# Channel mix with rows of 512 instead of 513, and a reordered opening, in a one-core RWKV and mixture-of-experts kernel

## The reference, cut to what matters

```
h0 = layernorm(x)
# attention part (time mix, then channel mix)
x1  = ln(h0; ln1_g, ln1_b);  xln = ln(x1; tm_g, tm_b);  xs = shift(xln)     # shift: row t takes row t-1, row 0 is 0
mix = xln * time_first + xs * (1 - time_first)
dec = exp(time_decay * (T - 1 - t))
v   = xln @ Wv;  vmix = sum_t v * dec;  x2 = h0 + sigmoid(mix @ Wr) * (vmix @ Wo + bo)
xc  = ln(ln(x2; ln2_g, ln2_b); cm_g, cm_b);  xcs = shift(xc)
kc  = relu(xcs @ Wck)^2                                                     # 512 -> 2048
x   = x + x2 + sigmoid(xc @ Wcr) * (kc @ Wcv)                               # 2048 -> 512
# ffn part: 32 experts, top 4 of them by groups, and a shared expert of 1024
out = x + routed_experts(layernorm(x)) + relu(h @ Wsu)^2 @ Wsd
```

## Time and profile before

| | |
|---|---|
| median of 3 executions | 1049.67 us (1048.85 to 1050.69) |
| the profiled execution | 1056.41 us, of which the span shown is 1054.7 us |
| TensorE busy | 1035.4 us (98% of the span) |
| VectorE, ScalarE, GpSimd busy | 656.1, 551.7, 428.4 us |
| mean granted TensorE clock | 0.997 |

### The profile page before, as it was taken

The page is one execution under the profiler, slowest core; times in us unless marked ns, Lnnn a source line. Parts: engine busy times, 40 slices in busy tenths (PEclk is TensorE's granted clock), DMA queues, the critical chain, the costliest instruction groups (busy, mean ns, idle before and its releaser), DMA issues.

```text
span 1054.7 us, 18034 instructions
## 1 busy us (share of the span) xinstructions
PE 1035.4 (98%) x5378; PEld 852.3 (81%) x5378; DVE 656.1 (62%) x1188; ACT 551.7 (52%) x944; POOL 428.4 (41%) x332
## 2 busy tenths in 40 slices
PE   6999999999999999999999999989999999999998
PEld 2556888888788878887887888879999999999986
DVE  7967948904590458041008398947777777777746
ACT  5963546333433343333345443347777777777742
POOL 1021304221222122202223423367778888888532
PEclk9999999999999999999999999989999999999999
DMA  9905296516421643334264891066988989988688
GB/s 291 384 9 196 90 346 207 176 60 241 160 99 60 239 159 99 99 120 160 100 213 154 292 298 71 1 214 129 260 193 254 237 193 323 218 163 167 93 283 343
DMA packets 102389, 195.05 MB, mean 185 GB/s; under 512 B 15544, under 2 KB 39096, under 8 KB 101824
## 3 DMA queue, kind: packets, MB, share of 16 engines
q1 hardware_dynamic: 82944, 158.70, 43.3%
q0 software_dynamic: 18816, 34.64, 17.3%
q10 hardware_dynamic: 576, 1.05, 0.4%
HBM read 141.98 MB, written 63.18 MB: 195 GB/s over the span
## 4 chain that ended last, share of the span: by engine, by line
PE 91%; DVE 4%; issue 2%; ACT 1%; DMA 1%; POOL 1%; POOLq 0%; ACTq 0%; DVEq 0%
PE bank L683 42%; PE bank L1018 23%; PE bank L1637 14%; PE bank L588 5%; PE bank L1627 3%; DMA tdb<-in_L_attn_time_decay 1%; PE bank L1029 1%; PE bank L1039 1%; PE bank L1089 1%; POOL mix_lo L395 0%; DVE bns L257 0%; DVE hb L854 0%; PE bank L642 0%; PE bank L625 0%; DVE mx L384 0%
## 5 line engine op out<-in xcount | busy, mean ns | idle before, releaser
L995 POOL TENSOR_TENSOR ksp_lo<-ra,ksp_hi 128x512 fp32r<-128x512 f32 x94 | 140.3, 1492 | 435.6 <-ACT ksp_hi L938 435.4
L1637 PEld LDWEIGHTS bank<-xT,wus 128*128 128x128 f32 x1344 | 163.8, 192 | 7.2
L1637 PE MATMUL bank<-xT,wus 128*128 128x128 f32 x1344 | 164.3, 276 | 0.0
L1018 PE MATMUL bank<-vring,ksp_hi 128*128 128x512 f32 x512 | 159.4, 393 | 0.0
L930 ACT ACTIVATE ra<-bank 128x512 f32<-128x512 f32 x96 | 57.4, 598 | 173.8 <-PE bank L683 169.5
L1789 DVE TENSOR_TENSOR wd_lo<-w,wd_hi 128x1024 fp32r<-128x1024 f32 x84 | 103.0, 1226 | 49.0 <-ACT wd_hi L1717 30.8
L683 PE MATMUL bank<-wd_hi,aT 128*128 128x512 f32 x336 | 126.8, 418 | 4.0 <-DVE aT L1783 4.0
L938 ACT ACTIVATE ksp_hi<-ra 128x512 fp32r<-128x512 f32 x96 | 60.7, 632 | 120.0 <-PE bank L1018 119.5
L1018 PEld LDWEIGHTS bank<-vring,ksp_hi 128*128 128x128 f32 x512 | 95.5, 188 | 20.0
L683 PE MATMUL bank<-xcT_hi,wck_lo 128*128 128x512 f32 x256 | 101.7, 397 | 0.0
L683 PE MATMUL bank<-xcT_lo,wck_hi 128*128 128x512 f32 x256 | 101.5, 396 | 0.0
(11 more groups left out here) (293 smaller groups left out, 2081.6 us busy)
## 6 DMA issues: line engine op xcount, KB each, us to landing
vring<-wcv_d SPq DMA_DIRECT2D x64, 512.0 KB, 3.3
w<-in_L_ffn_Wu SPq DMA_DIRECT2D x32, 512.0 KB
w<-in_L_ffn_Wd SPq DMA_DIRECT2D x32, 512.0 KB
hT_d<-hT SPq DMA_DIRECT2D x16, 512.0 KB, 3.9
hTb<-hT_d SPq DMA_DIRECT2D x3, 2048.0 KB
raw_wcv<-in_L_attn_Wcv SPq DMA_DIRECT2D x4, 1024.0 KB, 6.9
raw_wck<-in_L_attn_Wck SPq DMA_DIRECT2D x4, 1024.0 KB, 9.6
add_d<-zrow SPq DMA_DIRECT2D x1, 4096.0 KB, 20.4
```

What stands on the lines that cost most here:

```text
L995: nc.gpsimd.tensor_tensor(ksp[1][:, i % 2], ra[:, i % 2], ksp[0][:, i % 2], ALU.subtract).then_inc(sem("klo_in"), 1)
L1018: m = nc.tensor.matmul(bank[to + j][:], ksp[l][:, i % 2, j * P:(j + 1) * P], rhs(r), start=i == 0 and k == 0, stop=i == last and k == 2)
L1637: m = nc.tensor.matmul(bank[4 + u][:, n * P:(n + 1) * P], wus[u][:, c * EI + n * P:c * EI + (n + 1) * P], xT4[:, u, c * P:(c + 1) * P], st ...
```

## The change

It has two parts.

**Channel mix.** `xcT` becomes one tile [128, 2, 4, 512] with rows of exactly 512 elements. A row holds the shifted block only: element 0 from the block before, elements 1 to 511 the first 511 elements of this block. The last 128 elements of the block, which the gate product of j = 3 needs, go to a new tile `xc3` [128, 2, 4, 128] by a second ScalarE copy and a second VectorE subtraction for each chunk. The gate products of j = 0 to 2 still start at element 1 + 128 j. The last element of a block goes through a small tile `carry` (a VectorE copy after the subtractions, and one ScalarE copy before the next block's), instead of two ScalarE copies inside `xcT`. The semaphores hiT_in and loT_in count 2 for a chunk. As `xc3` shares memory with `tmp`, VectorE waits for the gate products of block 0 before it starts the front of block 1.

**Opening.** ln1_g and ln1_b are issued by SyncE after tile 0 of x, not by ScalarE. A one-element Exp on `ages` comes ahead of the wait for `tdb`, and brings the function table's load with it. `act_norm(act, 0)` moves between the two `act_stats`. `pe_idle` issues 11 matmuls instead of 12.

```diff
+        xcT_t = at("xcT", [P, 2, C, BLK], R, 136)
+        xcT = [xcT_t[:, s] for s in range(2)]
+        xc3 = at("xc3", [P, 2, C, P], R, 186)
+        carry = at("carry", [P, 2, C], R, 152.0625)
-        xcT = [at(f"xcT_{s}", [P, C, BLK + 1], R, 136 + 8.0625 * n) for n, s in enumerate(("hi", "lo"))]
...
         def stage1_scalar(act):
             act.dma_start(f1_flat[:, 1:2], x_pairs[0][:, 1:2]).then_inc(sem("x1_in"), 16)
-            for n, v in enumerate(("ln1_g", "ln1_b")):
-                act.dma_start(g1b[:, n], vec(f"L0_attn_{v}")).then_inc(sem("g1_in"), 16)
             act.dma_start(tdb[:], vec("L0_attn_time_decay")).then_inc(sem("tdb_in"), 16)
             act.wait_ge(sem("ages_in"), 1)
+            nc.scalar.activation(warm[:], ages[:, 0:1], ACT.Exp, scale=0.0)
             act.wait_ge(sem("tdb_in"), 16)
             for t in range(2):
                 act_decay(act, t)
             act_stats(act, 0, 4)
+            act_norm(act, 0)
             act_stats(act, 2, 6)
-            act_norm(act, 0)
...
-            pe_idle(pe, 12)
+            pe_idle(pe, 11)
...
         def stage1_sync(sp):
             sp.dma_start(f1_flat[:, 0:1], x_pairs[0][:, 0:1]).then_inc(sem("part_in0"), 16)
+            for n, v in enumerate(("ln1_g", "ln1_b")):
+                sp.dma_start(g1b[:, n], vec(f"L0_attn_{v}")).then_inc(sem("g1_in"), 16)
             sp_x(sp, 1)
...
             wait_apart(dve, sem("x2_in"), 32 if isinstance(b, int) else 16 * b + 16)
+            if isinstance(b, int) and b:
+                dve.wait_ge(sem("rcp_in"), BT)
...
         def dve_lo_xc(dve, b, first=False):
             for c in range(C):
-                dve.wait_ge(sem("hiT_in"), b * C + c + 1)
-                nc.vector.tensor_tensor(xcT[1][:, c, 1:BLK + 1], bank[...][:], xcT[0][:, c, 1:BLK + 1],
+                rows = bank[TURNED[-1][c] if first else 6 + c % 2]
+                dve.wait_ge(sem("hiT_in"), 2 * (b * C + c + 1))
+                nc.vector.tensor_tensor(xcT[1][:, c, 1:], rows[:, 0:BLK - 1], xcT[0][:, c, 1:],
                                         ALU.subtract).then_inc(sem("loT_in"), 1)
+                nc.vector.tensor_tensor(xc3[:, 1, c], rows[:, BLK - P:], xc3[:, 0, c],
+                                        ALU.subtract).then_inc(sem("loT_in"), 1)
+            wait_apart(dve, sem("loT_in"), 2 * (b * C + C))
+            nc.vector.tensor_copy(carry[:], xc3[:, :, :, P - 1]).then_inc(sem("carry2"), 1)
...
         def act_hi_xc(act, b, first=False):
             act.wait_ge(sem("trT_in"), b * C + 1)
             if first:
-                act.wait_ge(sem("carry2"), 2)
+                act.wait_ge(sem("carry2"), 1)
             else:
-                for s in range(2):
-                    nc.scalar.activation(xcT[s][:, :, 0:1], xcT[s][:, :, BLK:BLK + 1], ACT.Copy).then_inc(sem("carry2"), 1)
-                act.wait_ge(sem("carry2"), 2 + 2 * b)
+                act.wait_ge(sem("carry2"), 2 * b)
+                nc.scalar.activation(xcT_t[:, :, :, 0], carry[:], ACT.Copy).then_inc(sem("carry2"), 1)
+                act.wait_ge(sem("carry2"), 2 * b + 1)
             for c in range(C):
                 act.wait_ge(sem("trT_in"), b * C + c + 1)
-                nc.scalar.activation(xcT[0][:, c, 1:BLK + 1], bank[...][:], ACT.Copy).then_inc(sem("hiT_in"), 1)
+                rows = bank[TURNED[-1][c] if first else 6 + c % 2]
+                nc.scalar.activation(xcT[0][:, c, 1:], rows[:, 0:BLK - 1], ACT.Copy).then_inc(sem("hiT_in"), 1)
+                nc.scalar.activation(xc3[:, 0, c], rows[:, BLK - P:], ACT.Copy).then_inc(sem("hiT_in"), 1)
...
-            pe.wait_ge(sem("loT_in"), b * C + C)
+            pe.wait_ge(sem("loT_in"), 2 * (b * C + C))
...
-                split_product(bank[6 + j % 2][:], lambda s, c: xcT[s][:, c, 1 + j * P:1 + (j + 1) * P],
+                split_product(bank[6 + j % 2][:], lambda s, c: xc3[:, s, c] if j == BT - 1 else xcT[s][:, c, 1 + j * P:1 + (j + 1) * P],
...
-                pe_inner_up(pe, b * NCI + i, i % 4, [m[i // 4] for m in wck], lambda s, c: xcT[s][:, c, 0:BLK])
+                pe_inner_up(pe, b * NCI + i, i % 4, [m[i // 4] for m in wck], lambda s, c: xcT[s][:, c])
```

More of the change, by code:

```diff
@@ L149, in program @@
         r2 = at("r2", [P, NT], F, 184.8125)
+        warm = at("warm", [P, 1], F, 185.75)
         nm2 = at("nm2", [P, NT], F, 184.875)
@@ L832, in dve_lo_xc @@
             for c in range(C):
-                dve.wait_ge(sem("hiT_in"), b * C + c + 1)
-                nc.vector.tensor_tensor(xcT[1][:, c, 1:BLK + 1], bank[TURNED[-1][c] if first else 6 + c % 2][:], xcT[0][:, c, 1:BLK + 1],
+                rows = bank[TURNED[-1][c] if first else 6 + c % 2]
+                dve.wait_ge(sem("hiT_in"), 2 * (b * C + c + 1))
+                nc.vector.tensor_tensor(xcT[1][:, c, 1:], rows[:, 0:BLK - 1], xcT[0][:, c, 1:],
                                         ALU.subtract).then_inc(sem("loT_in"), 1)
+                nc.vector.tensor_tensor(xc3[:, 1, c], rows[:, BLK - P:], xc3[:, 0, c],
+                                        ALU.subtract).then_inc(sem("loT_in"), 1)
+            wait_apart(dve, sem("loT_in"), 2 * (b * C + C))
+            nc.vector.tensor_copy(carry[:], xc3[:, :, :, P - 1]).then_inc(sem("carry2"), 1)
         def dve_tail_a(dve, b):
@@ L869, in stage2_vector @@
             dve.wait_ge(sem("z_in"), (NB - 1) * BT)
-            for s in range(2):
-                nc.vector.memset(xcT[s][:, :, 0:1].bitcast(F), 0.0).then_inc(sem("carry2"), 1)
+            nc.vector.memset(xcT_t[:, :, :, 0].bitcast(F), 0.0).then_inc(sem("carry2"), 1)
             dve_lo(dve, "wcv1")
@@ L903, in act_hi_xc @@
             if first:
-                act.wait_ge(sem("carry2"), 2)
+                act.wait_ge(sem("carry2"), 1)
             else:
-                for s in range(2):
-                    nc.scalar.activation(xcT[s][:, :, 0:1], xcT[s][:, :, BLK:BLK + 1], ACT.Copy).then_inc(sem("carry2"), 1)
-                act.wait_ge(sem("carry2"), 2 + 2 * b)
+                act.wait_ge(sem("carry2"), 2 * b)
+                nc.scalar.activation(xcT_t[:, :, :, 0], carry[:], ACT.Copy).then_inc(sem("carry2"), 1)
+                act.wait_ge(sem("carry2"), 2 * b + 1)
             for c in range(C):
                 act.wait_ge(sem("trT_in"), b * C + c + 1)
-                nc.scalar.activation(xcT[0][:, c, 1:BLK + 1], bank[TURNED[-1][c] if first else 6 + c % 2][:], ACT.Copy).then_inc(sem("hiT_in"), 1)
+                rows = bank[TURNED[-1][c] if first else 6 + c % 2]
+                nc.scalar.activation(xcT[0][:, c, 1:], rows[:, 0:BLK - 1], ACT.Copy).then_inc(sem("hiT_in"), 1)
+                nc.scalar.activation(xc3[:, 0, c], rows[:, BLK - P:], ACT.Copy).then_inc(sem("hiT_in"), 1)
         def act_rc(act, b):
@@ L1086, in pe_turn_xc @@
             if c >= 2 and not opening:
-                pe.wait_ge(sem("loT_in"), b * C + c - 1)
+                pe.wait_ge(sem("loT_in"), 2 * (b * C + c - 1))
             for j in range(BT):
```

## The result

The changed kernel takes 1044.20 us (median of 5 runs, 1043.95 to 1044.87) against 1049.91 (5 runs, 1048.85 to 1050.69) for the kernel before: ratio 0.9947, 95% interval 0.9934 to 0.9959. The forecast was 1043.0 with 1041.0 to 1047.0. The profiled execution took 1044.20 (span 1042.4).

A forecast was written before the change was run, and what follows sets the result against it. The prediction took TensorE, busy for 98% of the span, to bound the kernel. Its terms -6.2 - 0.3 + 0.9 + 0.1 - 1.2 = -6.7 us took 1049.67 to 1043.0, with 8 in 10 held by 1041.0 to 1047.0.

The forecast's parts named there:

- Up products and gates: Channel mix: aligned rows bring up products from 2.81 to 2.72 us, -6.2; only the fourth gate speeds up, -0.3.
- Block 0: First gate of the channel mix: TensorE waits for VectorE's added narrow subtractions, +0.9, bounds +0.5 to +1.3.
- The other borders: Starts of blocks 1 to 3: VectorE's longer work just fits, +0.1 for the three together, bounds 0 and +0.9.
- The opening: Start of the kernel: TensorE starts tile 0 earlier, then waits for tile 4's norm; -1.2, bounds -0.8 and -2.1.
- I expect them before 8.1 and that wait gone: Opening: both norm vectors land from SyncE's queue before 8.1 us, ending VectorE's 0.59 us wait for ln1_b.
- tile 4 would be late next: Opening: TensorE would be due at tile 4 at 37.2 us, but ScalarE's norm has it ready at 38.0.
- The lower bound: Opening, -0.8: if ln1_b lands no earlier, ScalarE keeps its times and TensorE uses up tile 4's 0.8 us slack.
- The step from the profiled execution to the median by a difference: Whole kernel: profiled 1056.41 lies 6.7 above the plain median; the saving carries over, so 1049.67 - 6.7.
- the rows aren't the reason: Rival, channel mix: `xcT` and its weights collide wherever they lie; only opening and waits count, 1049.5 us; chance 0.09.
- half the gain: Rival, up products: only unaligned chunks or only `lo` pay less, so half of 6.2 goes, 1046.1 us; chance 0.09.
- The clock: Rival, opening: TensorE's wait at tile 4 drops the clock to 1.2 GHz, +3.3, 1046.3 us; chance 0.04.
- The new place: Rival, up products: `hi` and `lo` 8 KB apart make operand streams collide at every matmul, 1057.5 us; chance 0.04.

The follow-up runs named there:

- rows_only: The change's channel mix part alone, with the opening of the kernel before: 1044.56 us, ratio 0.9949 to the kernel before.
- xcT_64: The changed kernel with `xcT` alone moved by 64 bytes: 1050.36 us in one execution, against 1050.90 for the kernel before on its chip.
- xcT_256: The changed kernel with `xcT` alone moved by 256 bytes: 1046.46 us in one execution, against 1050.90 for the kernel before on its chip.
- wide_first: The changed kernel with block 0's four wide subtractions before the narrow ones, awaited only ahead of the fourth gate: 1048.86 us (second chip), ratio 0.993 to the kernel before.
- ln1_back: The changed kernel with both ln1_g and ln1_b loads back at the head of ScalarE's queue, ahead of `tdb`: 1044.33 us, ratio 0.9945 to the kernel before.
- ln1_split: The changed kernel with ln1_g loaded on ScalarE's queue ahead of `tdb` and ln1_b on SyncE's: 1044.55 us, ratio 0.9946 to the kernel before.
- opening_only: The change's opening edits alone, with the channel mix keeping rows of 513: 1050.15 us, ratio 1.000 to the kernel before.
- combined: The changed kernel with block 0's wide subtractions first, ln1 loads back on ScalarE's queue, and `hTb`'s first load issued earlier: 1043.78 us, ratio 0.993 to the kernel before.
- stride528: The kernel before with `xcT` rows padded from 513 to 528 elements, data from element 0: 1057.29 us in one execution, against 1056.03 on its chip.

## Why the prediction was right, step by step

**Up products and gates: right, in mechanism and in size.** Forecast -6.2 and -0.3. From first gate to first gate, and to the last product, the four blocks are shorter by 1.54, 1.45, 1.46 and 1.50: -5.95 together against -6.5. The gates did what was said, nearly: three of four still take 2.79, the fourth 2.76 and not 2.72. The reason given, that the new tile is laid out as `hTb` is, holds; it is finer than "the row's length" or "where a row starts": what counts is the offset of `xcT`'s rows against what else TensorE reads. The rule from the page "TensorE: Matmul & The Clock Gate" of the Trainium skill, section "Step-by-step: what each phase is for", by which only the number of columns counts, would have given a time within 0.2% of before; with the same columns `rows_only` is 5.7 us faster than before, and `xcT_64`, which differs from `xcT_256` in an offset alone, takes 5.53 a pair against 5.44 (3.9 us in all, by one execution each). The measurement decides.

**Block 0: the right wait, over-sized.** Forecast +0.9 (bounds +0.5 to +1.3), measured +0.42, just outside, between the time mix's first gate product and block 0's (55.04 before, 55.46 after); the gap itself is 0.79 instead of 0.23. The term that was too big is the narrow subtraction: its record says 0.28, but the next instruction starts 0.20 behind it (136.58 to 136.78), and behind a wide one, whose record says 0.69, it starts after 0.61. A record's duration overlaps with the next record; the pace has to be taken from start to start. The row of the first gate names "issue" and not VectorE, as was forecast; that it was VectorE is shown by `wide_first`.

**The other borders: right** at the lower bound; no wait.

**The opening: wrong.** Forecast -1.2 with bounds of -0.8 and -2.1, measured +0.49. The step that failed first is "I expect them before 8.1 and that wait gone": `ln1_b` was there at 9.4. With it came the rest: ScalarE's norm of tile 0 starts at 18.37 where 16.9 was forecast, and that of tile 4 at 38.61 where 37.14 was, both 1.47 later. TensorE's first pass starts at 21.82 and not at 19.6. That tile 4 would be late next was right: the pass due at 39.13 (38.70 + 0.43) starts at 39.48.

The lower bound failed too, and this is the flaw of the new order. It took ScalarE to keep its times if `ln1_b` lands no earlier. But the norm of tile 0, which waits for VectorE's `nm` and so for `ln1_b`, now stands in front of the second round of statistics. In eight of the nine traces with the new opening the norm of tile 4 starts 29.12 or 29.13 behind the idle matmuls, and in all nine the first pass on tile 4 starts later than its pace: 0.53 to 2.40 behind the pass before, where 0.43 is the pace. In the five with the old opening it never does. With the same landing (8.62 in `ln1_back`, 8.64 before) the rest of the opening's edits gives 0.49 at tile 4 and 0.39 at the first gate product. The size is loose: from the start of the idle matmuls to tile 4 the old opening takes 30.01 to 30.57 in five traces, the new one 29.98 to 30.00 in those eight.

And the term was over-sized even with the vectors in time: `ln1_split` meets that condition and gives 0.57. ScalarE's work up to the norm of tile 4 took 0.3 longer than was worked out, with a second wait for `nm` (0.20) in it, and tile 4, which was put at 39.26 in the kernel before, starts there at 39.09.

**Not in the forecast: what stage 3 takes and gives back.** The wait for `hTb` grew by 0.70 (gap 0.91 to 1.61). Against this the wait for `hb`, 1.05 before, went, since VectorE's writes no longer met GpSimd: -0.4 in sum. And a gain in the opening would not have come through in full: `ln1_back` is 0.80 ahead of the changed kernel at the end of stage 2 and 0.39 at stage 3's first product.

Sum: -6.7 forecast; 0.5 less from the products, 0.5 better at block 0, 0.1 at the borders, 1.7 lost in the opening, 0.4 won in stage 3: -5.5 from the traces up to the expert stage, -5.7 between the medians. That the time came out only 1.2 above the forecast is in part luck: the opening missed by 1.7, outside its bounds, and 0.9 came back: 0.5 from block 0, and 0.4 from stage 3, of which the working says nothing. One bound of the range was also added up wrongly: the borders at +0.9 make 1043.8, not 1045. The step from the profiled execution to the median by a difference held, because the 6.7 us lie in one place, and the rows aren't what decides about them: with the old rows `opening_only` waits only 1.20 there and keeps the full clock.

**The rivals.** That the rows aren't the reason is refuted by `rows_only`, and, free of the other edits of the channel mix, by `xcT_64` against `xcT_256`; half the gain would have been 2.81 for some of the products, and all are at 2.72. The clock stays at 1.00 behind the wait at tile 4. The new place isn't worse, and the distance of 8 KB between `hi` and `lo` does no harm.

## What to carry to other kernels

Take the pace of one kind of instruction from start to start and compare it between stages: two streams of the same shape that differ by 3% can tell of a layout. Lay the tiles that TensorE reads in one stretch of work out with rows at equal offsets, and don't spend an element in front of a row for a shift. Before work is spent on an early stage, look for the next transfer with a time of its own (here `hTb`, issued late for no need), and behind it for the next engine: in `combined` the wait moved from `hTb` to `hb` and from there to `aT`.

## What the runs showed of the hardware

- In a row of products on tiles at the same offset, 12 matmuls of 512 columns took 2.72 us, also with everything shifted by 64 bytes or `xcT` alone by 256. With `xcT` at other offsets up products took 2.75 to 2.82 and gates, where it is the stationary operand, 2.76 to 2.80; an up product and the down product behind it took 5.49 to 5.54 instead of 5.44.
- Three transfers that repeat one row of 2 KB over all partitions (256 KB each) are spread out, on one queue or on two: they land 5.4, 6.8 and 9.1 us after their issue on ScalarE's queue before; 6.3 beside 5.6 and 7.7 on two queues after.
- VectorE's scale and shift of 512 elements out of SBUF had a record of 0.54 us alone, and of 1.52 and 2.60 where an operation of GpSimd ran beside it; both ended 0.29 behind that operation.
- At the start of the expert stage TensorE waited 4.00 us in the profiled execution of before and the granted clock was 0.50, the 1.2 GHz level, from 706.5 to 713 us. The four traces of the second chip show the same, with old rows and with new: waits of 2.79 (`wide_first`), 3.33, 4.60 and 4.66, and a mean clock down to 0.74 in `wide_first` from 700 to 706.5 and to 0.53 in `stride528` from 706.5 to 713. In the nine other traces no wait there is over 1.20, and the clock stays at 1.00. The second chip takes 6 us more for the kernel before in all 9 runs. Why the wait is longer there wasn't settled.
